# A graph attention kernel on one core: the edge stages' sums by pairs of tiles, with more messages and a ring of one-hots

## What is computed

```python
xp = (x @ W).reshape(-1, Hh, C)
alpha = a_src[src] + a_dst[dst] + a_edge
alpha = jax.nn.leaky_relu(alpha, NEG_SLOPE)
m = jax.lax.stop_gradient(jax.ops.segment_max(alpha, dst, num_segments=n_nodes))
ex = jnp.exp(alpha - m[dst])
denom = jax.ops.segment_sum(ex, dst, num_segments=n_nodes)
alpha = ex / (denom[dst] + 1e-16)
msg = xp[src] * alpha[:, :, None]
out = jax.ops.segment_sum(msg, dst, num_segments=n_nodes)
```

## Time and profile before

| What | Value |
|---|---|
| Median of three runs | 3738.2 us (3726.09 to 3741.85) |
| The profiled execution's own time | 3723.76 us |
| Its span | 3722.0 us |
| Edge stage of layer 0, about | 177 to 1605 us |
| Edge stage of layer 1, about | 1762 to 3140 us |
| Granted clock, mean | 0.782 |

### The profile page before, as it was taken

The page is one execution under the profiler, slowest core; times in us unless marked ns, Lnnn a source line. Parts: engine busy times, 40 slices in busy tenths (PEclk is TensorE's granted clock), DMA queues, the critical chain, the costliest instruction groups (busy, mean ns, idle before and its releaser), DMA issues. The chain is left out here.

```text
span 3722.0 us, 60054 instructions
## 1 busy us (share of the span) xinstructions
PE 2531.6 (68%) x15613; PEld 2146.8 (58%) x15614; DVE 2126.3 (57%) x6066; ACT 1171.6 (31%) x4747; POOL 2014.2 (54%) x2269
## 2 busy tenths in 40 slices
PE   6467667666676767683666666666666666859898
PEld 4355555555565556562555555555555555638787
DVE  6355555555555655652555555555555556766565
ACT  3133333333333333351222222222222224522222
POOL 3555555555555555535555555555555554726665
PEclk8677777778777777896777777777777777869999
DMA  9544444444444444314444444444444443545433
GB/s 255 153 119 119 116 122 117 120 117 128 114 126 121 123 120 126 109 64 117 134 121 136 125 129 134 125 135 126 138 126 133 131 124 87 165 134 160 151 114 96
DMA packets 282397, 475.71 MB, mean 128 GB/s; under 512 B 69124, under 2 KB 191644, under 8 KB 282116
## 3 DMA queue, kind: packets, MB, share of 16 engines
q0 software_dynamic: 96912, 288.68, 28.2%
q1 hardware_dynamic: 120884, 137.12, 12.2%
q10 hardware_dynamic: 64320, 46.56, 4.0%
HBM read 398.47 MB, written 75.78 MB: 127 GB/s over the span
## 5 line engine op out<-in xcount | busy, mean ns | idle before, releaser
L707 POOL DMA_INDIRECT e_rows<-table,e_idx x1664 | 1578.9, 949 | 1305.0 <-DVE e_msg L747 950.3
L1087 PE MATMUL e_ps_sum<-e_hot,e_msg 128*128 128x129 f32 x6656 | 1358.4, 351 | 871.5 <-ACT parts L943 477.3
L1087 PEld LDWEIGHTS e_ps_sum<-e_hot,e_msg 128*128 128x128 f32 x6656 | 1138.1, 247 | 1028.1 <-issue 604.9
L942 ACT ACTIVATE acc<-e_ps_sum 128x256 f32 x1664 | 641.2, 385 | 1931.3 <-PE e_ps_sum L1087 814.4
L726 DVE TENSOR_TENSOR e_hot<-e_ps_pr,rel 128x512 f32<-128x512 f32 x416 | 285.5, 686 | 829.0 <-PE e_ps_sum L1087 406.7
L747 DVE TENSOR_TENSOR e_msg<-e_rows,e_ps_pr 128x256 f32<-128x256 f32 x1664 | 654.7, 414 | 40.0 <-remote 5.3
L943 ACT ACTIVATE parts<-e_ps_sum 128x4 f32<-128x4 f32 x1664 | 281.0, 169 | 0.0
L1069 PE MATMUL e_ps_al<-e_dst_score,e_hotT 128*128 x3328 | 217.6, 179 | 52.1 <-issue 44.4
L1069 PEld LDWEIGHTS e_ps_al<-e_dst_score,e_hotT 128*128 128x128 bf16 x3328 | 199.3, 103 | 81.4 <-issue 51.2
L737 DVE TENSOR_SCALAR e_hotT<-e_relb,pcolf 128x512 bf16<-128x512 bf16 x416 | 144.6, 348 | 38.9 <-issue 23.9
L2281 ACT ACTIVATE x_h<-x,eb 128x128 f32<-128x128 f32 x216 | 67.7, 364 | 273.6 <-PE x L2355 227.5
(11 more groups left out here) (370 smaller groups left out, 3400.3 us busy)
## 6 DMA issues: line engine op xcount, KB each, us to landing
e_relb<-rel_rows SPq DMA_DIRECT2D x104, 512.0 KB
e_rows<-table,e_idx POOLq DMA_INDIRECT x1664
e_eattr<-in_edge_b SPq DMA_DIRECT2D x104, 128.0 KB
e_xT<-turned_x ACTq DMA_DIRECT2D x100, 128.0 KB
e_xr<-in_x ACTq DMA_DIRECT2D x100, 128.0 KB
node<-l_row SPq DMA_DIRECT2D x25, 512.0 KB, 3.1
table<-t_row SPq DMA_DIRECT2D x25, 276.0 KB
table<-j_row SPq DMA_DIRECT2D x25, 276.0 KB, 2.4
```

The source lines that it names most:

```text
L707: nc.gpsimd.indirect_dma_start(out=rows[q][:, k, :], out_offset=None, in_=table[0:NP], in_offset=bass.IndirectOffsetOnAxis(ap=idx[:, q, k: ...
L942: nc.scalar.activation(acc[:, :, bass.ds(at[k], P)], ps_sum[(k + q) % 3][:, :, 0:P], ACT.Copy).then_inc(s["window"], 1)
L1087: op = nc.tensor.matmul(ps_sum[(k + q) % 3][:, a, 0:WIN], msg[:, k % RM, a * P:a * P + P], hot[:, q, k, :], start=(a == 0), stop=True, ski ...
```

## The change

`ps_sum` holds two tiles in a bank: the window has 128 columns, of which the last is the mark of the last destination. `totals(g, k)` makes two tiles' sums with one wait for messages, one for `taken` and one signal, and `windows` empties two tiles and takes their parts with one instruction of 128x8. Three banks thus hold six tiles. `msg` has 14 slots. `hot` is a ring of five slots of four tiles, filled by `one_hots` one quarter group at a time for the group that uses it, at k = 1, 5, 9 and 13; it waits for the pair of totals 16 tiles before the ones that it serves. The turned one-hots are `turned_hots`, at k = 3, 6, 14 and 15, and `scores` runs at 9, 10, 14 and 15. The steps of the softmax and of the blocks stand at other tiles, the block steps of group g now in steps g to g+2. The diff, cut to these parts:

```diff
     parts, src_sb, rel, islast = v["parts"], v["src_sb"], v["rel"], v["islast"]
     first_sb, row_iota, wedge = v["first_sb"], v["row_iota"], v["wedge"]
     table = v["table"][layer]
-    RM = 8
+    RM = 14
+    RH = 5
...
         eattr = tmp("eattr", [P, 2, 2, P])
-        hot = tmp("hot", [P, 2, GT, WIN])
+        hot = tmp("hot", [P, RH, 4, P])
         hotT = tmp("hotT", [P, 2, 2, 4, P], BF16)
         relb = tmp("relb", [P, 2, GT, P], BF16)
         mark = tmp("mark", [P, 2, 2, WIN], BF16)
...
         turned_al = ps_al[:, NPC * GT:NPC * GT + P]
         run, ex, iota = ([ps[:, P * c:P * c + P] for ps in ps_pr] for c in (0, 1, 3))
-        ps_sum = [pb(f"e{layer}_ps_sum{q}", [P, 2, F], ctx) for q in range(3)]
+        ps_sum = [pb(f"e{layer}_ps_sum{q}", [P, 2, 2, P], ctx) for q in range(3)]
...
-            def one_hots(g, q, r, i, c):
-
-                if not isinstance(g, int) or g > 1:
-
-                    vec.wait_ge(s["sum"], 16 * g + 4 * r - 12)
+            def one_hots(g, r, c):
+
+                slot = (4 * g + r) % RH
+                if 4 * g + r >= RH:
+                    vec.wait_ge(s["sum"], 8 * g + 2 * r)
+                nc.vector.tensor_copy(hot[:, slot, :, P - 1:P], islast[:, bass.ds(g * GT + 4 * r, 4)].unsqueeze(2))
+                nc.vector.tensor_tensor(hot[:, slot, :, 0:P - 1], iota[c][:, 0:P - 1].unsqueeze(1).broadcast_to((P, 4, P - 1)),
+                                        rel[:, bass.ds(g * GT + 4 * r, 4)].unsqueeze(2).broadcast_to((P, 4, P - 1)), ALU.is_equal)
+
+            def turned_hots(g, q, r, i):
+
                 if r == 0:
                     vec.wait_ge(s[f"rel{q}"], 16 * i + 16)
-                if r == 3:
-                    nc.vector.tensor_copy(hot[:, q, :, P:P + 1], islast[:, bass.ds(g * GT, GT)].unsqueeze(2))
-                nc.vector.tensor_tensor(hot[:, q, 4 * r:4 * r + 4, 0:P], iota[c].unsqueeze(1).broadcast_to((P, 4, P)),
-                                        rel[:, bass.ds(g * GT + 4 * r, 4)].unsqueeze(2).broadcast_to((P, 4, P)), ALU.is_equal)
-
-                if r == 0:
-                    if not isinstance(g, int) or g > 0:
+                    if g > 0:
                         vec.wait_ge(s["part"], 3 * g)
                 elif r == 1:
                     vec.wait_ge(s["scores"], g + 2)
-                vec.wait_ge(s["sum"], 16 * g + 16 + k - RM + 1)
+                if k % 2 == 0:
+                    vec.wait_ge(s["sum"], 8 * g + k // 2 + 9 - RM // 2)
                 nc.vector.tensor_tensor(
-                    msg[:, k % RM, :].rearrange("p (h c) -> p h c", c=C),
+                    msg[:, (16 * g + k) % RM, :].rearrange("p (h c) -> p h c", c=C),
                     rows[q][:, k, 0:F].rearrange("p (h c) -> p h c", c=C),
...
+                    if layer == 0 and 0 < g <= NB:
+                        if k == 5:
+                            keys_centred(g - 1)
+                        if k == 13:
+                            keys_scales(g - 1)
+                    if layer == 1 and k == 5 and 0 < g <= NB:
+                        mixed(g - 1, p, (g - 1) // 2)
+                    if k in (1, 5, 9):
+                        one_hots(g, {1: 1, 5: 2, 9: 3}[k], q)
+                    if softmax and k == 13:
+                        one_hots(n, 0, q)
+                    if ahead and k in (3, 6, 14, 15):
+                        turned_hots(g + 2, q, {3: 0, 6: 1, 14: 2, 15: 3}[k], i + 1)
+                    if softmax and k == 4:
                         leaky(n, p, i if p == 1 else i + 1, more=ahead)
                     if softmax and k == 7:
...
-                    if ahead and k == 9:
-                        one_hots(g + 2, q, 1, i + 1, q)
                     if softmax and k == 10:
                         running(n, p)
                     if softmax and k == 11:
                         whole(n, p)
                     if softmax and k == 12:
                         inverse(p)
-                    if softmax and k == 13:
                         probability(n, p)
-                    if ahead and k == 14:
-                        one_hots(g + 2, q, 2, i + 1, q)
...
-            def window(g, q, k, at):
-
-                act.wait_ge(s["window"], 16 * g + k + 1)
-                act.wait_ge(s["sum"], 16 * g + 16 + k + 1)
-                nc.scalar.activation(acc[:, :, bass.ds(at[k], P)], ps_sum[(k + q) % 3][:, :, 0:P], ACT.Copy).then_inc(s["window"], 1)
-                nc.scalar.activation(parts[:, bass.ds(g * GT + k, 1)].rearrange("p t a b -> p (t a) b"),
-                                     ps_sum[(k + q) % 3][:, :, 0:P + 1:P], ACT.Copy).then_inc(s["taken"], 1)
+            def windows(g, k, at):
+
+                pair = 8 * g + k // 2
+                act.wait_ge(s["sum"], pair + 9)
+                for e in range(2):
+                    act.wait_ge(s["window"], 16 * g + k + e + 1)
+                    nc.scalar.activation(acc[:, :, bass.ds(at[k + e], P)], ps_sum[pair % 3][:, e], ACT.Copy).then_inc(s["window"], 1)
+                nc.scalar.activation(parts[:, bass.ds(g * GT + k, 2)].rearrange("p t a b -> p (t a) b"),
+                                     ps_sum[pair % 3][:].rearrange("p t a n -> p (t a) n")[:, :, 0:P:P - 1], ACT.Copy
+                                     ).then_inc(s["taken"], 1)
...
-                    window(g, q, k, at)
-                    if layer == 0 and (not isinstance(g, int) or 0 < g <= NB):
-                        if k == 1:
+                    if k % 2 == 0:
+                        windows(g, k, at)
+                    if layer == 0:
+                        if k == 5 and 0 < g <= NB:
+                            block_squares(g - 1, 1 - q, (g - 1) // 2)
+                        if k == 7 and 0 < g <= NB:
+                            store_block(g - 1, 1 - q)
+                        if k == 9 and 1 < g <= NB + 1:
+                            columns(g - 2)
+                        if k == 11 and 0 < g <= NB:
+                            rows_centred(g - 1, 1 - q, (g - 1) // 2)
...
+                    if softmax and k == 3:
                         exps(g + 1, 1 - q)
...
-            def total(g, q, k):
-                pe.wait_ge(s["msg"], 16 * g + 32 + k + 1)
-
-                pe.wait_ge(s["taken"], 16 * g + k + (2 if q == 0 and k < 2 else 1))
-                for a in range(2):
-                    op = nc.tensor.matmul(ps_sum[(k + q) % 3][:, a, 0:WIN], msg[:, k % RM, a * P:a * P + P], hot[:, q, k, :],
-                                          start=(a == 0), stop=True, skip_group_check=True)
+            def totals(g, k):
+                pair = 8 * g + k // 2
+                pe.wait_ge(s["msg"], 16 * g + 32 + k + 2)
+
+                pe.wait_ge(s["taken"], pair + 1)
+                for e in range(2):
+                    for a in range(2):
+                        op = nc.tensor.matmul(ps_sum[pair % 3][:, e, a], msg[:, (16 * g + k + e) % RM, a * P:a * P + P],
+                                              hot[:, (4 * g + k // 4) % RH, (k + e) % 4], start=(e == 0 and a == 0), stop=True,
+                                              skip_group_check=True)
...
+                    if k % 2 == 1:
+                        totals(g, k - 1)
+                    if layer == 0:
+                        if k == 5 and 1 < g <= NB + 1:
+                            key_sums(g - 2)
+                        if k == 15 and block_too:
+                            keys(g, q, i)
+                    elif block_too:
+                        if k == 5:
+                            turn_squares(g, q, i)
+                        if k == 15:
+                            mix(g, q, i)
+                    if softmax and k == 4:
                         turn_alpha(n)
+                    if softmax and k == 12:
                         turn_prob(n, p)
+                    if ahead and k in (9, 10, 14, 15):
+                        scores(m, q, {9: 0, 10: 1, 14: 2, 15: 3}[k], j)
```

More of the change, by code:

```diff
@@ L917, in _ @@
             probability(0, 0)
-            for r in range(3):
-                one_hots(1, 1, r, 0, 1)
+            for r in range(4):
+                turned_hots(1, 1, r, 0)
             if layer == 1:
@@ L1038, in _ @@
                 step(g, g % 2, g // 2)
+            step(NG - 1, 1, NG // 2 - 1, softmax=False)
             if layer == 0:
```

66 lines of the change are left out of this document (18 added, 48 removed).

## The result

The changed kernel took 3556.8 us (median of six runs, 3547.8 to 3578.0), the kernel before 3733.2 us beside it: a ratio of 0.953, 95% interval 0.9508 to 0.9552. The forecast was 3384 us; the change gained 176 us where 354 were expected. So there are two questions: why the gain was half in the first measurement, and what it hangs on.

What follows compares the result with a forecast made beforehand. Engines waiting in turn, mostly VectorE at the one-hots, bound the kernel. Steps falling from 27.5 to 24.1 and 26.5 to 23.1 us save 177 us per layer, 354 off 3738.2: 3384 us, range 3110 to 3700.

Steps and rivals of the forecast that it cites:

- What bounds the kernel: Edge stages: no engine fills a 27 us step; engines wait in turn, VectorE mostly at one-hots; gathers need 20.0 us.
- The ring: At the one-hots: waiting 14 tiles back instead of one or two removes 8.0 us a step (layer 0), 9.7 (layer 1).
- the wait of L814: VectorE's 1.3 us a step ahead of L814 should go, since PE's product now comes in the step before.
- What is late next: After the one-hots, the queue of gathers; part of 8.0 us returns at turned scores, turned probabilities and turned one-hots.
- The size of a step: Edge stages: good steps of the kernel before plus 0.6 us of copies, 24.1 us in layer 0 and 23.1 in layer 1.
- two of its signs of being wrong: Rests of PE, VectorE and ScalarE over 5 us; VectorE waiting over 4 us a step for the turned scores.
- The rival of one pause a step: PE's late signal after the scores stops VectorE once a step: 25.6 us a step, 3593 us; chance 0.20.
- The gathers as the bound: Rival: clock up and no stall, the queue of gathers sets 21.0 us a step, 3115 us; chance 0.15.
- Copies of 128x4: On VectorE, four copies for one a step, costing between nothing and 0.6 us more; 0.6 taken.
- ScalarE's early wait for `less`: After tile 3, ScalarE's later windows queue behind it: priced at nothing, up to 5.2 us a step if PE's signals are late.
- The clock: PE's granted clock in the edge stages should rise from 0.77 and 0.75 to over 0.85 with fewer stalls.

Runs made afterwards that it cites:

- `sums_before`: The kernel before, with the sums' signals awaited at the one-hots made late through SyncE by two small transfers: 3772.8 us, ratio to the kernel before 1.265.
- `after_again`: The changed kernel unaltered, run again beside the kernel before in a later group: 2993.7 us, ratio to the kernel before 1.0034.
- `sums_after2`: The changed kernel with the one-hots' sum signals late by two small transfers, relayed one step earlier: 3607.5 us beside 3763.9 for the kernel before, ratio 0.9585.

## Why the prediction was half right

**What bounds the kernel: right.** Engines waiting in a circle, VectorE at the one-hots, the floor of the gathers at 20.0 us: with prompt signals both kernels run at 20.3 to 20.5 us a step.

**The ring: right as a removal.** 8.0 us a step ahead of the one-hots went to nothing, as did the wait of L814 (L818 now: 0.0). `sums_before` shows that a late sum is enough to make such waits.

**What is late next: named in part, mis-sized.** "So of 8.0 us a part returns as waits there" was the step that failed. All of it returned in idleness of VectorE, 4.3 + 3.8 us, and 2.2 of 7.5 us a step were won on the path. Of the places that the prediction named only the turned one-hots hold much (4.3 us). At the turned scores VectorE waits 8.6 / 45.2 = 0.2 us a step (L778), at all the messages 22.9 / 45.2 = 0.5. The other 3.8 us stand at L767, the first read of the scores, which the prediction did not name and where nothing was waited for before. So two of its signs of being wrong, over 4 us at the turned scores and rests of over 5 us, did not come; the wait of that size stood at a neighbouring point.

**The size of a step: wrong by the choice of the sample.** I took the good steps of the kernel before, 23.5 and 22.5 us, as what a step would cost. But in layer 0 a good step stood beside one of 33 us, 56.8 us for the pair or 28.4 each, and in layer 1 the mean of 26.5 shows that 22.5 was an exception. That a short step is short because the gathers ran ahead during the long one is my reading, not shown; that it was no fair sample is. The changed kernel's steps are 25.3 and 25.4 us on the average, against 24.1 and 23.1 forecast. (1.2 + 2.3) x 51.94 is 182 us; forecast and result lie 173 apart.

**The rival of one pause a step: nearly the outcome.** It gave 25.6 us a step and 3593 us, and 25.3, 25.4 and 3557 were measured. Its mechanism was there too, VectorE stopped a few tiles ahead of late scores, only as two smaller pauses (2.84 and 1.78 us in the step shown) rather than one of 5.90. That its time came within 1% is partly luck, since two pauses of another size made it up. I had held the good steps against it, the same error as in the sum.

**The gathers as the bound: right elsewhere.** It gave 21.0 us a step. With prompt signals it is 20.4, and for the kernel before as well, so that the change wins nothing there: a ratio of 1.0034. "The trace does not show the cause of the lateness" should have become a rival of its own: that without the lateness the kernel before is already at the floor.

**Small terms.** Copies of 128x4: 34.0 / 45.2 = 0.75 us a step against 0.2 before, so 0.55 for the 0.6 forecast. ScalarE's early wait for `less`, priced at nothing: it waits 100.4 us in 1200, which holds up PE nowhere: among PE's waits none for ScalarE's parts is left. The clock: over 0.85 was forecast and 0.77 came. The Trainium skill (TensorE: Matmul & The Clock Gate, HAM oscillation) has waits that recur in each round bring PE to its low clock; the trace agrees, since the waits were still there, two in each step, and the clock was 0.77 and 0.72 where it had been 0.77 and 0.75.

## What to carry to other kernels

An idle time that an edit removes comes back at the next wait for the same late thing: look for every wait on that engine's signals, not for the largest one, and lengthen them together, since two waits in a row can be one chain. Never take the good half of an alternating pair as the cost of a step. And where a wait is long because a signal comes late for no reason that the profile shows, run the unchanged kernel again, in several groups of runs, before building on it; a relay through an idle engine then shows what a few microseconds of lateness at each wait are worth.

## What was not expected of the hardware

The same program took 3733 us in the first measurement and 3764 us in the last group, and 2979 to 2986 us in the four between, 25% apart, each within 0.6% of its median. Durations of instructions were the same in both (a gather 953 ns against 947, a message 414 ns); what differed was when PE's signals came. The first measurement and the last group show it alike. Where ScalarE had waited for a sum, the changed kernel's window began 1.95 us (median) after the sum's modelled end in the first measurement and 0.12 us in `after_again`. VectorE's signals were not late: where POOL had waited for a message, its gather began 0.27 us after the message's end (median of the first measurement, in both kernels).

The records differ as well. Of the 9048 semaphore updates that the changed kernel's instructions make, at least 1907 are not on record in the first measurement and 2014 in `sums_after2`, against 9 in `after_again`; for the kernel before it is 2026 of 10712 against 6. Those of layer 0's scores, counted above, are complete. So late signals and lost records come together, and whether the recording itself has a part in the lateness was not tried.

In the first measurement some steps of the changed kernel, of about 30 us and about seven steps apart, also show PE issuing the scores' products one by one, 2.1 us apart, with "issue" as what it waited for:

```profile
866.07 0.18 PE L1074 MATMUL e_ps_al<-e_dst_score,e_hotT 128*128 x1 [1.91 <-issue]
868.18 0.18 PE L1074 MATMUL e_ps_al<-e_dst_score,e_hotT 128*128 x1 [1.93 <-issue]
870.27 0.18 PE L1074 MATMUL e_ps_al<-e_dst_score,e_hotT 128*128 x1 [1.91 <-issue]
```

In the prompt runs no two products of one set started over 1 us apart; in the changed kernel of the first measurement 53 did. The cause of the lateness stays open: register addresses and the gathers in flight were each a theory, and the two runs made for them fell where no signal was late.
